# Embedding bag on one core: the columns of the lookups of features 1 to 19 are made in the second half of the first feature, one operation behind each chunk

## The reference

```python
B, F, V, L, E = (512, 32, 12500, 20, 64)
emb = flat[ids + offs]                                  # (B, F, L, E), f32
mask = (jnp.arange(L_) < lengths[..., None]).astype(emb.dtype)
pooled = jnp.einsum('bfle,bfl->bfe', emb, mask)
out = pooled.reshape(Bq, F_ * E_)
return jnp.nan_to_num(out)
```

## Time and profile before

| | |
|---|---|
| median of 3 runs | 1046.8 us (1046.41 to 1047.93) |
| profiled execution, its own time | 1047.35 us |
| its span | 1045.4 us |
| PE busy | 983.3 us, 94% |
| DVE busy | 937.4 us, 90% |
| ACT busy | 754.1 us, 72% |
| POOL busy | 666.0 us, 64% |
| chain that ended last | PE 79%, DVE 16%, ACT 2% |
| largest waits of PE | `pairs` for DVE's `onehot_j`: 28.3 us in 17 waits, the longest 6.8 |

### The profile page before, as it was taken

One profiled execution on the slowest core, in us unless ns is written; L12 is line 12 of the kernel. 1 busy time (PEld: TensorE's weight loads), 2 busy tenths in 40 slices (PEclk: granted clock), 3 DMA queues, 4 the chain that ended last, 5 costly groups with the idle time before them and its releaser, 6 DMA issues.

```text
span 1045.4 us, 29010 instructions
## 1 busy us (share of the span) xinstructions
PE 983.3 (94%) x9885; PEld 864.1 (83%) x9885; DVE 937.4 (90%) x2485; ACT 754.1 (72%) x1121; POOL 666.0 (64%) x617
## 2 busy tenths in 40 slices
PE   3499999999999999999999999999999999999996
PEld 0188888888888888888888888888888888888885
DVE  9987879898999989999989998999999898999980
ACT  2477777878686868787777777787868686877770
POOL 3874677676676756777667767767676775773010
PEclk9999999999999999999999999999999999999998
DMA  6234142534444343535252626244443434241300
GB/s 220 82 136 118 37 141 67 152 111 131 128 120 135 115 141 105 161 86 179 69 171 76 188 59 191 75 148 119 129 133 115 146 106 116 76 115 50 106 28 6
DMA packets 66140, 119.85 MB, mean 115 GB/s; under 512 B 31600, under 2 KB 33351, under 8 KB 66065
## 3 DMA queue, kind: packets, MB, share of 16 engines
q1 hardware_dynamic: 45696, 100.66, 30.0%
q0 software_dynamic: 19168, 17.93, 8.5%
q10 hardware_dynamic: 1200, 0.58, 0.2%
HBM read 83.45 MB, written 4.71 MB: 84 GB/s over the span
## 4 chain that ended last, share of the span: by engine, by line
PE 79%; DVE 16%; ACT 2%; issue 1%; DVEq 1%; POOL 0%; POOLq 0%
PE sums L530 55%; PE pairs L520 18%; PE rest L548 6%; DVE onehot_j L746 5%; DVE gathered L804 3%; DVE onehot_p L744 2%; ACT table L487 1%; DVE table L755 1%; DVE table L763 1%; ACT counts L475 1%; DVEq L800 1%; DVE is_nan L772 0%; DVE gathered L775 0%; DVE counts L636 0%; DVE j_of L688 0%
## 5 line engine op out<-in xcount | busy, mean ns | idle before, releaser
L530 PE MATMUL sums<-table,counts 128*128 128x192 bf16 x7840 | 806.7, 247 | 0.0
L475 ACT ACTIVATE counts<-pairs 128x588 int16<-128x588 f32 (+1 forms) x880 | 563.7, 651 | 239.5 <-PE pairs L520 232.8
L530 PEld LDWEIGHTS sums<-table,counts 128*128 128x128 fp8e3 x7840 | 690.1, 96 | 44.4 <-issue 0.2
L432 POOL DMA_INDIRECT rows<-tables,row_now x495 | 553.3, 1118 | 245.6 <-PE pairs L520 128.9
L746 DVE TENSOR_SCALAR onehot_j<-ramp,j_of,worth 128x296 bf16<-128x296 f16 x1680 | 491.9, 355 | 0.0
L520 PE MATMUL pairs<-onehot_j,onehot_p 128*128 128x294 bf16 x1720 | 364.6, 292 | 40.6 <-DVE onehot_j L746 28.3
L520 PEld LDWEIGHTS pairs<-onehot_j,onehot_p 128*128 128x128 bf16 x1720 | 159.5, 97 | 101.0 <-issue 27.9
L744 DVE TENSOR_TENSOR onehot_p<-ramp,p_of 128x768 bf16<-128x768 f16 x280 | 153.7, 549 | 72.7 <-PE pairs L520 71.9
L804 DVE TENSOR_REDUCE gathered<-rows 128x64 f32<-128x1280 f32 x48 | 114.3, 2381 | 3.5 <-issue 3.5
L442 POOL DMA_INDIRECT out_gathered<-gathered,place_now x48 | 52.4, 1091 | 69.3 <-issue 67.1
L548 PE MATMUL rest<-table,minus_eye 128*128 128x448 bf16 x320 | 91.5, 367 | 3.6 <-ACT rest L483 1.6
(11 more groups left out here) (67 smaller groups left out, 83.3 us busy)
## 6 DMA issues: line engine op xcount, KB each, us to landing
table<-tables SPq DMA_DIRECT2D x140, 448.0 KB
rows<-zeros SPq DMA_DIRECT2D x48, 640.0 KB
rows<-tables,row_now POOLq DMA_INDIRECT x495
out_counted<-pooled SPq DMA_DIRECT2D x120, 21.0 KB
rows<-lookup_ids SPq DMA_DIRECT2D x1, 817.0 KB, 8.2
rows<-lookup_lengths SPq DMA_DIRECT2D x1, 817.0 KB, 9.7
sorted_records<-records,rank POOLq DMA_INDIRECT x48
out_gathered<-gathered,place_now POOLq DMA_INDIRECT x48
```

The source lines that it names most:

```text
L432: nc.gpsimd.indirect_dma_start(out=rows[:, k, l * E:(l + 1) * E], out_offset=None, in_=table_rows, in_offset=bass.IndirectOffsetOnAxis(ap= ...
L475: nc.scalar.activation(dst, src, ACT.Copy).then_inc(counts_saved, 1)
L530: last = nc.tensor.matmul(sums[h][:, k * PARTS * E:(k + 1) * PARTS * E], counts[h][:, j, :, k], parts[:, :, j, :, 1], start=(j == 0 and k ...
```

## The change

The seven operations become seven numbered steps of `column_step(halves, n)`. For feature 0 all seven run where they ran. For features 1 to 19 step n runs behind chunk n of feature 0's second half; the wait for the lookups' loads moves ahead of step 0, and `lookups_read` is raised behind step 6, which is behind that half's chunk 6.

```diff
--- before.py
+++ after.py
@@ -111,6 +111,7 @@
     BODIES = TILES // BUFFERS
     STAGES = 2 * CHUNKS
     assert TILES % BUFFERS == 0 and BUFFERS % 2 == 0 and BODIES > 1
+    assert CHUNKS == 7
     assert J % CHUNKS == 0 and GROUPS * GROUP >= HALF and PER_CHUNK % 2 == 0 and CHUNKS * PER_CHUNK == LAST
     assert STAGES % AHEAD == 0 and P_COLUMNS % 2 == 0 and L < 32 and LAST_BAGS == 4 and 2 * EVICTIONS % SETS == 0
     assert L % 4 == 0 and TRIO * L <= 64 and WIDE <= 512 and HALF == 2 * P and 2 * PARTS * E <= 512
@@ -675,20 +676,29 @@
                 step(nc.vector.tensor_scalar(arrival[:], arrival_f, 16.0, None, ALU.mult))
                 dve.sem_inc(depths_ready, 1)
 
-            def columns_of_lookups(halves):
+            def column_step(halves, n):
 
                 part = columns(halves)
                 a, b = work_a[:, part], work_b[:, part]
-                step(nc.vector.tensor_scalar(a, look_id[:, part], 1.0 / J, 0.5 / J - 0.5, ALU.mult, ALU.add))
-                step(nc.vector.tensor_scalar(b, a, MAGIC, MAGIC, ALU.add, ALU.subtract))
-                nc.vector.tensor_copy(p_of[:, halves, 0:GROUPS], b.rearrange("p (h g) -> p h g", g=GROUPS))
-                step(nc.vector.scalar_tensor_tensor(out=a, in0=b, scalar=-float(J), in1=look_id[:, part],
-                                                    op0=ALU.mult, op1=ALU.add))
-                step(nc.vector.tensor_scalar(b, a, float(TRIO), place[:, 1:2], ALU.mult, ALU.add))
-                step(nc.vector.scalar_tensor_tensor(out=j_of[:, part], in0=look_len[:, part], scalar=place[:, 0:1], in1=b,
-                                                    op0=ALU.is_gt, op1=ALU.mult))
-                last = j_of[:, part].rearrange("p (h g) -> p h g", g=GROUPS)[:, :, LAST]
-                step(nc.vector.tensor_scalar(last, last, back_a_slot[:], None, ALU.add))
+                if n == 0:
+                    step(nc.vector.tensor_scalar(a, look_id[:, part], 1.0 / J, 0.5 / J - 0.5, ALU.mult, ALU.add))
+                if n == 1:
+                    step(nc.vector.tensor_scalar(b, a, MAGIC, MAGIC, ALU.add, ALU.subtract))
+                if n == 2:
+                    nc.vector.tensor_copy(p_of[:, halves, 0:GROUPS], b.rearrange("p (h g) -> p h g", g=GROUPS))
+                if n == 3:
+                    step(nc.vector.scalar_tensor_tensor(out=a, in0=b, scalar=-float(J), in1=look_id[:, part],
+                                                        op0=ALU.mult, op1=ALU.add))
+                if n == 4:
+                    step(nc.vector.tensor_scalar(b, a, float(TRIO), place[:, 1:2], ALU.mult, ALU.add))
+                if n == 5:
+                    step(nc.vector.scalar_tensor_tensor(out=j_of[:, part], in0=look_len[:, part], scalar=place[:, 0:1], in1=b,
+                                                        op0=ALU.is_gt, op1=ALU.mult))
+                if n == 6:
+                    last = j_of[:, part].rearrange("p (h g) -> p h g", g=GROUPS)[:, :, LAST]
+                    step(nc.vector.tensor_scalar(last, last, back_a_slot[:], None, ALU.add))
+
+            COLUMN_STEPS = CHUNKS
 
             def weigh_lookups():
 
@@ -714,9 +724,13 @@
                     rows_of_block(c)
                 elif c == BLOCKS:
                     find_depths()
-                elif c == BLOCKS + 1:
+
+            def prepare_columns(c):
+
+                if c == 0:
                     dve.wait_ge(other_lookups_in, 32)
-                    columns_of_lookups(OTHER_HALVES)
+                column_step(OTHER_HALVES, c)
+                if c == COLUMN_STEPS - 1:
                     dve.sem_inc(lookups_read, 1)
 
             ramp_twice = ramp[:, 0:2 * P].rearrange("p (n x) -> p n x", x=2)
@@ -839,7 +853,8 @@
             count_lengths()
             negate_eye()
             dve.wait_ge(first_lookups_in, 32)
-            columns_of_lookups(FIRST_HALVES)
+            for n in range(COLUMN_STEPS):
+                column_step(FIRST_HALVES, n)
 
             for f in range(M):
                 for h in range(2):
@@ -847,6 +862,8 @@
                         chunk(f, h, c)
                         if f == 0 and h == 0:
                             prepare(c)
+                        if f == 0 and h == 1:
+                            prepare_columns(c)
 
             for t in range(LEFT, TILES):
                 add_rows(t)
```

## The result

The changed kernel takes 1049.01 us (median of 12 runs, 1048.57 to 1050.33); the kernel before, in 12 runs beside it, 1046.86 (1046.09 to 1047.93). The ratio is 1.0021, with a 95% interval of 1.0012 to 1.0030: slower by 2.15 us, where 2.5 faster was forecast. The profiled execution of the changed kernel took 1048.89 us, its span is 1047.0.

The account below looks back on a forecast made before the run. PE was taken to set the pace; it begins feature 1 6.2 us earlier, but a load behind the fills stops it 3.7 us, leaving 2.5 of gain: 1046.8 - 2.5 = 1044.3 us, range 1042.0 to 1046.5.

Parts of the forecast that it names:

- What bounds the kernel: PE sets the pace in the long middle, busy 94% of the span; feature 0 only moves the steady part's start.
- both moves of the columns: Feature 0: first products 7.3 us earlier without the columns; with them in the second half, PE begins feature 1 6.2 earlier.
- That the fills stand ahead of the load and PE stops for it: Feature 1's first load queues behind eight fills of zeros; PE stands 3.7 us, leaving 2.5 us of gain.
- The load's 448 KB at the same 344 GB/s are 1.3 us more: it has landed at 86.5, 16.7 us behind the semaphore.: Feature 1's first table load: fills drained at 85.2, then 1.3 us for its bytes, landing at 86.5.
- The bound of 1.2 us: Allowance for the semaphore or the fills coming later than thought, which would leave a gain of 1.3 us.
- It decides from a stall of about 4.3 us on: PE's stop at feature 1: the long clock fall decides from about 4.3 us, if the load lands at 87.1 or later.
- the cases that I had given 0.13 together: The clock falls while PE stands at feature 1: briefly, 1046.4 us, chance 0.08; or long, 1049.0 us, chance 0.05.
- The third rival: Clock falls at PE's stop in feature 1 and stays low 9.4 us, costing 4.7: 1049.0 us, slower; chance 0.05.
- the second rival: Clock falls at PE's stop in feature 1 and soon returns, costing 2.1 us: 1046.4 us, no change; chance 0.08.
- The first rival: Feature 1's first load doesn't wait for all the fills, so the whole 6.2 us stay: 1040.6 us; chance 0.10.
- the last (DVE's broken overlap): Second-half column steps cost 0.3 us more each on DVE, semaphore 2.1 us later: 1046.4 us, no change; chance 0.05.
- Costs put at nothing: Gathers waiting for later fills, POOL's scatter sharing DMA engines with the fills, and the seven steps' branch: no cost.

Follow-up runs that it names:

- The spread fills: Changed kernel with four of the eight fills of zeros kept in place, the others one behind each of feature 1's first four loads; 1040.61 us, ratio 0.9939.
- control: Changed kernel with feature 1 written out ahead of PE's loop and nothing else; 1049.42 us, ratio 1.0028 against the kernel before.
- the first load alone: Changed kernel where SP waits until feature 1's first load has landed before issuing the second; 1048.57 us, ratio 1.0015 against the kernel before.
- PE kept busy: Changed kernel with feature 1 written out ahead of PE's loop and 110 unread matmuls put before PE's wait; 1046.96 us, ratio 1.0002.
- seven fills: Changed kernel with seven fills of zeros ahead of feature 1's first load and one behind it; 1046.73 us, ratio 1.0002 against the kernel before.
- With six: Changed kernel with six fills ahead of feature 1's first load, two behind that load and the next; 1254.0, 1246.5, 1244.9 us, on slower chips only.
- The late fills in the kernel before: Kernel before, columns left in the first half, SP also waiting for a PE count so fills go out late; 1046.74 us, ratio 1.0000.

## Why the prediction was wrong

**What bounds the kernel, both moves of the columns: right.** 37.61, 44.99, 69.9 and 71.70 stand against 37.7, 44.8, 69.8 and 71.6; PE's wait at the last chunk was 0.83 instead of 1.1. PE did come 6.1 us earlier.

**That the fills stand ahead of the load and PE stops for it: right.** The spread fills show that it is they, with 8.4 us between two kernels that differ in nothing but their order.

**The term that failed first: "The load's 448 KB at the same 344 GB/s are 1.3 us more: it has landed at 86.5, 16.7 us behind the semaphore."** It was 18.5 to 19.7 us in four executions (the changed kernel, its control, the first load alone, PE kept busy), so 1.8 to 3.0 more. The page of the changed kernel gives 3.5 us as the median from a table load's issue to its landing, over all 140 loads; only 1.3 of these are its bytes. I took the rest to be hidden by the time in the queue. In the one profile where the load waited for the fills, the fills took 16.3 us (I had 15.4) and the load 3.66 (I had 1.3), so most of what was missing is the load's own time. And at the passage from fills to loads the full DMA engines moved 207 to 281 GB/s for some 2 us (229 from 82 to 84 with seven fills), which costs about 0.8 us against 371; whether this is the load's own start seen in the rate, or a loss beside it, isn't settled. With 3.5 in place of 1.3 the landing would have been 88.7, inside what was measured. With this term right, PE would have gone on at 89.8: a gain of 0.3, and no forecast of "faster". The bound of 1.2 us that I gave this term was too narrow, since nothing in the rows had shown the case and I named only the bytes.

**The step that failed next: "It decides from a stall of about 4.3 us on".** The one fall in the trace of before came 4.3 us behind the last matmul, and I made a threshold of one observation. The falls came 2.6 us behind PE's last matmul in the changed kernel, 3.6 with the first load alone, some 4.0 with seven fills and 5.1 in the control. A stop of 3.8 us was enough; one of 1.2 us was not. So the cases that I had given 0.13 together were the likely ones even with my own landing. This step alone takes 1.5 of the 2.5 us of gain, which would leave 1045.8; the seven fills took 1046.7, and the last 0.9 us of that isn't explained.

**The rivals.** The third rival's time, 1049.0, was met to 0.01 us, but that is luck, since its terms are wrong: it had a landing at 87.1 and 4.7 us of the clock, which was to stay down long; measured are a landing at 89.6, 0.5 us later than ACT once came for it, and 1.3 us of clock (1.2 to 2.3 in the other kernels). That is nearer the second rival's fall, priced there at 2.1, together with a load later than any rival had it. The load alone takes the whole gain and 0.5 us more, and the clock adds its 1.3. The first rival (the load doesn't wait) and the last (DVE's broken overlap) are refuted: the load landed 9.84 us behind its issue and not 3.3, and the steps in the second half cost DVE what the block had cost, the semaphore came at 69.9.

**Costs put at nothing** were nothing: in the kernel with spread fills the gathers run and the whole gain of 6.2 us is in the time, though four fills there go out as late as 75.8 to 86.2.

**The range.** Its lower end was to be half way between the forecast and the first rival. That is 1042.4 and not 1042.0; nothing hangs on it.

## What to carry to other kernels

When a step moves, list what its semaphore releases, and put the released transfers beside the ones that the consumer now wants earlier: a block of transfers in a queue costs nothing until the engine behind it becomes faster. A load behind a full queue is to be charged with its whole time from issue to landing, not with its bytes alone. And a stop of PE is to be priced with the low clock on top: here stops of 3.8 to 6.9 us brought it, at 1.2 to 2.3 us, and a stop of 1.2 us did not. A single fall seen in a trace gives no threshold.

## What the runs showed that I had not expected

The granted clock fell between 2.6 and 5.1 us behind PE's last matmul, and neither this time nor the price goes with the length of the stop. The price is a little under half of the time that PE then worked at the low level, as the prediction had reckoned; that time differed. In us, the fall and the time at the low level estimated from the granted clock of stretches of 1 us:

| kernel | stop of PE | fall behind the last matmul | PE at work at the low level | cost |
|---|---|---|---|---|
| seven fills ahead | 3.79 | 4.0 | 3.4 | 1.5 |
| first load alone | 5.38 | 3.6 | 5.1 | 2.3 |
| control, feature 1 written out | 5.77 | 5.1 | 2.8 | 1.2 |
| changed kernel | 6.49 | 2.6 | 2.9 | 1.3 |

With seven fills the clock fell at about 87.7, when PE had already gone on at 87.54. With six, and a stop of 1.18 us, it did not fall.

The rate of full DMA engines falls to nearly half for some 2 us where transfers from SBUF to SBUF end and loads from HBM begin in the same queue: 207 GB/s from 85 to 86 in the changed kernel, 229 from 82 to 84 with seven fills, with a share of 0.98 to 1.01, against 371 and 380 before it. The late fills in the kernel before show it too (228 and 207 from 83 to 85). In the kernel before itself, where no load stands behind the fills, the rate held at 354 until they ended at 61. Why it falls, no run here shows.

Three chips of the set ran every kernel here a fifth slower, at a granted clock of 0.95 to 0.96 in the mean of the profiled executions, with stops of PE of up to 17 us where it has none on the other chips; a difference of 2 us can't be read there.
